# Comparing one-hots against a row in PSUM, with one PSUM bank less for the segment sums, in a graph-transformer layer

## The reference

```python
xn = layernorm(x)
# relational graph convolution, 16 relations, both directions
proj = einsum('ni,rio->rno', xn, W)               # W = Wf, then Wb
m = (proj[etypes, src] + bias) * inv_degree(dst)[dst]
gnn = segment_sum(m, dst, num_segments=n)         # and once more with src and dst swapped
x1 = x + (2 * xn @ loop_weight + self_bias) + gnn_fwd + gnn_bwd + mixer(xn)
out = x1 + mixture_of_experts(layernorm(x1))      # top 2 of 8 experts
```

## Time and profile before

| | |
|---|---|
| time, median of 3 runs | 2231.8 us (2223.73 to 2234.8) |
| span of the profiled execution, first to last instruction | 2062.0 us |
| mean granted TensorE clock over the span | 0.978 |
| TensorE busy | 1966.0 us (95%) |
| TensorE weight loads busy | 1360.8 us (66%) |
| VectorE busy | 1150.2 us (56%) |
| GpSimd busy | 993.8 us (48%) |
| ScalarE busy | 607.9 us (29%) |
| the 1760 matmuls of the 880 segment sums | 486.5 us |
| the 880 adds | 371.0 us |
| the 220 one-hot instructions | 151.5 us |
| the 832 gathers on GpSimd | 831.5 us |

### The profile page before, as it was taken

One profiled execution on the slowest core, in us unless ns is written; L12 is line 12 of the kernel. 1 busy time (PEld: TensorE's weight loads), 2 busy tenths in 40 slices (PEclk: granted clock), 3 DMA queues, 4 the chain that ended last, 5 costly groups with the idle time before them and its releaser, 6 DMA issues.

```text
span 2062.0 us, 27476 instructions
## 1 busy us (share of the span) xinstructions
PE 1966.0 (95%) x8235; PEld 1360.8 (66%) x8235; DVE 1150.2 (56%) x2484; ACT 607.9 (29%) x1262; POOL 993.8 (48%) x966
## 2 busy tenths in 40 slices
PE   7999999999999999999998889999999499999998
PEld 3446544456666666555565566888888488888897
DVE  4999991056666666444787668555558711111111
ACT  2332333322222222222433222222223722222243
POOL 0000001067777777777567777777762023333332
PEclk9999999999999999999999999999997699999999
DMA  8332235456666656666555454333332754544573
GB/s 293 156 143 98 108 153 229 173 182 196 190 185 191 191 188 193 208 212 206 183 159 175 142 159 139 103 101 102 97 95 82 264 166 113 130 112 122 131 197 73
DMA packets 134186, 326.97 MB, mean 159 GB/s; under 512 B 24576, under 2 KB 65184, under 8 KB 132768
## 3 DMA queue, kind: packets, MB, share of 16 engines
q1 hardware_dynamic: 80064, 199.64, 26.7%
q0 software_dynamic: 50688, 123.79, 23.6%
q10 hardware_dynamic: 3296, 1.80, 0.3%
HBM read 196.42 MB, written 128.71 MB: 158 GB/s over the span
## 4 chain that ended last, share of the span: by engine, by line
PE 84%; DVE 5%; DMA 5%; ACT 3%; issue 2%; POOL 1%; DVEq 0%; POOLq 0%
PE bank L690 31%; PE bank L772 16%; PE bank L1983 10%; PE bank L1994 9%; PE bank L1912 4%; PE bank L1903 4%; DMA arena<-table_bwd,arena 3%; PE bank L597 3%; PE bank L1841 1%; DVE arena L808 1%; POOL arena L745 1%; DVE arena L409 1%; DMA table_fwd<-arena 1%; PE bank L1952 1%; ACT arena L1710 1%
## 5 line engine op out<-in xcount | busy, mean ns | idle before, releaser
L690 PE MATMUL bank<-arena,work 128*128 128x512 f32 x1600 | 733.1, 594 | 2.5 <-ACT arena L683 1.5
L808 DVE TENSOR_TENSOR arena<-arena,bank 128x257 f32 x880 | 371.0, 422 | 370.9 <-PE bank L772 298.8
L772 PE MATMUL bank<-arena 128*128 x1760 | 486.5, 388 | 24.3 <-DMA arena<-table_bwd,arena 15.9
L745 POOL DMA_INDIRECT arena<-table_fwd,arena x416 | 419.9, 1009 | 144.7 <-issue 86.0
L745 POOL DMA_INDIRECT arena<-table_bwd,arena x416 | 411.6, 989 | 152.4 <-issue 81.7
L690 PEld LDWEIGHTS bank<-arena,work 128*128 128x128 f32 x1600 | 299.3, 190 | 278.7 <-issue 261.8
L683 ACT ACTIVATE arena<-bank 128x512 f32<-128x512 f32 x400 | 239.6, 599 | 702.8 <-PE bank L690 699.2
L772 PEld LDWEIGHTS bank<-arena 128*128 128x128 f32 x1760 | 317.1, 191 | 144.0 <-issue 110.0
L1053 POOL DMA_INDIRECT out<-xn,work x56 | 89.5, 1599 | 249.7 <-DVE xn L193 181.7
L754 DVE TENSOR_TENSOR arena<-cst,arena 128x512 f32<-128x512 f32 x220 | 151.5, 689 | 97.9 <-PE bank L690 97.9
L1727 ACT ACTIVATE arena<-bank,work 128x256 f32<-128x256 f32 (+1 forms) x280 | 120.8, 432 | 284.2 <-PE bank L1983 277.6
(11 more groups left out here) (323 smaller groups left out, 1589.5 us busy)
## 6 DMA issues: line engine op xcount, KB each, us to landing
table_fwd<-arena SPq DMA_DIRECT2D x100, 512.0 KB, 2.6
table_bwd<-arena SPq DMA_DIRECT2D x100, 512.0 KB, 3.2
arena<-in_W SPq DMA_DIRECT2D x35, 1024.0 KB, 5.7
arena<-in_W SPq DMA_DIRECT2D x2, 4096.0 KB, 13.9
arena<-table_fwd,arena POOLq DMA_INDIRECT x416, 3.1
arena<-table_bwd,arena POOLq DMA_INDIRECT x416, 2.8
work<-x_transposed SPq DMA_DIRECT2D x50, 128.0 KB, 3.6
mix_rows<-arena SPq DMA_DIRECT2D x25, 256.0 KB, 2.6
```

What stands on the lines that cost most here:

```text
L690: last = pe.matmul(ps[4 + s % 2][:, :], xT[t % 2][:, k * P:(k + 1) * P], ar(W_off[d] + k * 4096 + c * 512, 512), start=(k == 0), stop=(k = ...
L745: e.indirect_dma_start(msg[m % RING][:, 0:C], None, table[d], bass.IndirectOffsetOnAxis(ap=idx[d][:, j:j + 1], axis=0)).then_inc(s_ga[m % ...
L772: pe.matmul(ps[sum_bank(n)][:, 0:W], oh[n % OHS], msg_all[:, ds(place.pop(n), W)], start=True, stop=True).then_inc(s_sm, 1)
L808: vec.tensor_tensor(to, to, ps[sum_bank(n)][:, 0:W], ALU.add).then_inc(s_ac, 1)
```

## The change

The row that the one-hots compare is copied once into PSUM bank 7, and the one-hot instructions read it there. The places `loc` and the one-hots themselves stay in SBUF. Bank 7 leaves both rings of the sums: NARROW is banks 1 and 6, SEG is banks 2, 3 and 6. So sum n now waits for add n-2 with NARROW and for add n-3 with SEG. The first sum of the wide part, n = 284, goes to bank 6, where sum 283 was. In the last row step one add more is taken ahead of the wait for the transposed maxima, since only three banks are left that could hold sums that are not yet added.

```diff
+        iota_ps = ps[7][:, 0:P]
...
-        NARROW, SEG = (1, 6, 7), (2, 3, 6, 7)
+        NARROW, SEG = (1, 6), (2, 3, 6)
...
-            vec.tensor_tensor(oh_all[:, b:b + 4, :], iota.unsqueeze(1).broadcast_to(four),
+            vec.tensor_tensor(oh_all[:, b:b + 4, :], iota_ps.unsqueeze(1).broadcast_to(four),
                               loc[n // TE][:, c:c + 4].unsqueeze(2).broadcast_to(four),
                               ALU.is_equal).then_inc(s_oh, 1)
...
                 V.mark(vec.memset(kmax[:, :], -3.0e38))
+                V.link(vec.tensor_copy(iota_ps, iota))
                 e.wait_ge(s_pj, SLOTS)
...
-                    add_sums(e, rows_upto(t), rows_upto(t) + 2)
+                    add_sums(e, rows_upto(t), rows_upto(t) + (2 if t + 1 < NT else 3))
...
-                add_sums(e, rows_upto(NT - 1) + 2, M1E + 3)
+                add_sums(e, rows_upto(NT - 1) + 3, M1E + 3)
```

## The result

The changed kernel took 2237.95 us (median; 2230.27 to 2243.59) beside 2228.09 us of the kernel before (2222.77 to 2237.03), 20 runs each: a ratio of 1.0039, 95% interval 1.0028 to 1.0050, so some 9 us slower. The forecast was 2243.3 us with a range of 2232 to 2257.

A forecast was written before the change was run, and what follows sets the result against it. TensorE was taken to bound the forward sums and MLP, GpSimd's gathers 1042 to 1288 us. The terms 10.6 + 1.3 + 3.0 + 1.0 - 4.4 gave +11.5 us on 2231.8, so 2243.3 us, range 2232 to 2257.

The forecast's parts named there:

- two banks, 16 slots: Forward sums: in slots with three sums, the third waits for the add of the first; +10.6 us (9.3 to 12.3).
- row steps, sums 416 to 465: First nine row steps: with three banks, sums wait for adds and VectorE slips; +3.0 us (0 to 7.2).
- end, sums 660 to 879: Last sums of the kernel: with three banks, unequal gaps between adds make some sums late; +1.0 us (0 to 4.1).
- one-hots' own time, 687 ns: One-hot instructions on VectorE: 687 ns from SBUF, 682 ns with one PSUM input; taken as 0 (0 to -1 us).
- gathers beside one-hots: GpSimd's gathers beside one-hots, 820 to 982 us: with the row in PSUM they fall from 1.06 to 0.95 us.
- what that gives: Time returned by quicker gathers where GpSimd is the bound, 1042 to 1288 us: -4.4 us (0 to -8.2).
- three signs of being wrong: No wait in three-sum slots, gathers beside one-hots still 1.06 us or more, or row steps after the ninth growing too.
- Rival 2: No relief: a gather near one-hots is slow for another cause and stays slow; +15.9 us, 2248 us; chance 0.15.
- rival 1: Three-sum slots cost 9.3 us, row steps and end nothing, gathers return 8.2; +2.3 us, 2234 us; chance 0.20.
- rival 3: Each of 25 row steps passes 0.8 us on, so gathers wait for sums; +28 us, 2260 us; chance 0.10.
- rival 4: Gathers land earlier and return over 15.9 us of TensorE's idle time, 1042 to 1288 us; -6 us, 2226 us; chance 0.08.
- The runs lie 169.8 us above the span at the median: Whole kernel: timed runs were taken to exceed the profiled span by 169.8 us, turning a 2073.5 us span into 2243.3 us.

The follow-up runs named there:

- experiment 2: The changed kernel, but the one-hots read the row in SBUF again, with bank 7 still out of the rings: 2079.45 us, 1.0077 to before.
- experiment 3: The changed kernel, but in the 16 three-sum slots the first sum stands between the two halves of the projection slot: 2068.10 us, 1.0021 to before.
- experiment 4: The kernel before, but three later banks and the row in PSUM from sum 284 on, one add moved ahead of the maxima: 2061.47 us, 0.9991.
- experiment 1: The kernel before, unchanged, profiled and timed once more: 2063.22 us, span 2061.2 us.
- experiment 6: The kernel before, but only the ring of the forward sums cut to two banks, row in SBUF: 2228.58 us, 0.9995 to before.
- experiment 7: The kernel before, but only the later ring cut to three banks, row in SBUF, one add moved ahead of the maxima: 2236.17 us, 1.0037 to before.
- experiment 5: The changed kernel again, unchanged, timed beside the kernel before on one chip: 2238.63 us, 1.0047 to before.
- experiment 8: The kernel before, but three banks and the row in PSUM only from sum 464 to 855, one add moved ahead of the maxima: 2230.82 us, 1.0016.

## Why the prediction came out near

The chances put most on slower by over 0.5% (0.50), and 0.43 on within 0.5%. The interval of the first comparison, 1.0028 to 1.0050, lies within 0.5%, the others of the changed kernel across it. The forecast of +11.5 us met +9 to +11 on B. Its steps can be checked only on A, the machine whose rows it used, and most of them hold there. On B, where the times were taken, the sum comes out near with other parts in it: the early banks cost almost nothing, the later ones twice the forecast, and the row gives nothing back. That hit is luck.

| step | forecast | on A | on B |
|---|---|---|---|
| two banks, 16 slots | +10.6 (9.3 to 12.3) | +12.1 | some +3.5 at sum 280, 0 (-3.3 to +1.1) in the time |
| boundary, sum 284 | +1.3 | +1.2 | not told apart |
| row steps, sums 416 to 465 | +3.0 | +3.1 | not told apart |
| end, sums 660 to 879 | +1.0 | +1.0 | not told apart |
| three later banks in all | +4.0 | +4 | +8.2 (5.6 to 11.1) |
| one-hots' own time, 687 ns | 0 | 0 (685) | 0 (686) |
| gathers beside one-hots | 1.06 to 0.95 us | 1.007 to 0.946, mean | 1.004 to 0.953, mean |
| what that gives | -4.4 (0 to -8.2) | -5.3 | 0 (-3 to +4) |

On A the figures are differences of the starts of sums between two traces, experiment 2 against before for the banks, experiments 3 and 4 against 2 for the gathers. Two traces of the kernel before differ by 0.5 us or less at sums 284, 416, 465 and 609 and by 2 us at sum 660, so -5.3 carries that much. The stretches for which the prediction had no term of the banks, sums 284 to 416 and 465 to 660, moved by +2.1 and -2.4 us in experiment 2, nearly nothing together. What was to be seen came as said: 17 waits, the forward part up to sum 284 13 us longer for 12, gathers at 0.946 us for 0.95 in experiment 4. The steps past the ninth row step, sums 465 to 660, didn't grow, so none of the three signs of being wrong was seen on A. From sum 416 to 660, about the row steps to the MLP, experiment 3's kernel is 4.5 us shorter than before, where 1 to 2 was forecast; experiment 1 is 1.8 shorter with no change at all.

*The slots.* The mechanism holds, wait by wait. The term was sized 1.5 us too low: nine of the slots shift TensorE by 0.64 us each and three by 0.70, the prediction's own figures before it took 0.11 off each. What doesn't carry over to this place is the hand-over. In the row steps a load follows the add's end by 0.13 us; in all 16 slots it is 0.24. At the last slot the load so moved from 0.51 us ahead of the add's end to 0.24 us behind it, by 0.75 us, while TensorE's later work moved by 0.64. So in these twelve slots 0.11 us of the wait is hidden, which the prediction had assumed without a row, and its hand-over was 0.11 us too short.

*The gathers.* Gathers beside one-hots are held by 0.06 us on average and by up to 0.24 (experiment 2, 820 to 982 us), and the hold is gone when one input is in PSUM. The Trainium skill, in "SBUF — State Buffer", section "Who interferes with whom", has a VectorE instruction with two SBUF inputs contend with a GpSimd instruction that reads SBUF. The trace agrees, with 1.007 against 0.946 us, and the gathers do read SBUF: each takes its row numbers from `arena`. The Trainium skill also infers there that descriptor generation needs the write side, which `tensor_tensor` leaves free. These gathers were held all the same; whether in reading or in writing, no run here tells. Rival 2 (no relief) was wrong as a mechanism. On B it is right as a price: the gathers get shorter, but the time doesn't. GpSimd there waits for TensorE's sums (133.8 us for the backward gathers in the row above), which would leave nobody waiting for what it gains; that link is argued, not tested. The higher fixed cost for a PSUM source in the Trainium skill ("VectorE: DVE Perf Modes", section "The TRN2 errata") doesn't show in the changed kernel either: 686 ns against 687.

*The other rivals.* Waits half hidden (rival 1) fails on A, where the slots cost their full figure. Waits handed on (rival 3) would have added 20 us in the steps; A shows 3.1. A gain from the gathers' landing (rival 4) needed more than 15.9 us back; A shows 5.3.

*The sum on A.* Experiment 2 costs 16.3 us and the row gives 5.3 of them back: about +11, worked out and not run. Whole times give nearly the same: experiment 4's time with the 13.2 us of the early banks on top is about +11.5.

*The step that failed* is "The runs lie 169.8 us above the span at the median". Only 2 us lie outside the span (experiment 1), so a trace of 2062 us and times of 2232 us for one kernel should have stopped me. The reasoning on "TensorE is busy 394.86 of 395 us", "whatever holds TensorE there is paid in full" and "nothing takes it back" is true on A and false where the times were taken. On B TensorE idles 49 us in that stretch, what the forward sums' waits cost there is smaller and no longer seen at sum 416 (experiment 6), while the later three banks cost twice what was forecast (experiment 7).

*What stays open.* Why the delay of two banks is made good on B, and why three later ones cost 8 us, I can't show. That a fourth bank lets TensorE run past a late result, while the add of a third sum is awaited anyhow, would fit both; it is argued, not shown. Up to sum 280 the traces of experiments 5 to 8 agree to 0.3 us where the early banks are the same; behind it single traces on B scatter by several us (sum 416 starts 635.6 us after the first in experiment 6 and 640.2 in experiment 5, sum 879 1312.7 and 1317.4), as much as the parts in question, so only the timed ratios count there. The clock's part is not separated either: it is granted at 0.963 over the span of after and 0.979 in experiment 1.

## What to carry to other kernels

Compare the span of the profiled execution with the timed runs before anything else; if they differ by much more than the 2 us seen here, the trace and the times come from different conditions, and a sum built on "no idle time" in one need not hold in the other. A wait that a smaller ring adds can be priced from two rows, the end of what it will wait for and the start of what waits, but the time from the one to the other must be read at a place of the same kind: it was 0.13 us in the row steps and 0.24 in the slots. Moving one of the one-hots' two SBUF inputs to PSUM cost no time in the instruction and freed GpSimd's gathers, but it gained time only on A, where GpSimd was the bound for a stretch, and there less than the changed kernel's lost bank cost.

## What was not expected of the hardware

- The same kernel takes 2063, 2209 or 2228 us on the chips it fell on, each run within 0.5% of the median, and a change that gains 0.1% on one loses 0.6% on another.
- The slower chips' extra time begins with the gathers. Up to the first sum at 423 us the traces agree within 2 us; with three banks sum 284 then comes about 41 us later on B (experiments 7 and 8) and sum 879 about 170.
- There, results of TensorE reach ScalarE, VectorE and GpSimd late together, by 1 to 4 us, again and again. The DMA packets of a gather are no slower (2.8 us in the middle from issue to last packet in experiments 1 and 6), and what holds the results is in no record. Whether it is the chip or some other load on it wasn't tried.
